# A third layer's attention: steps of two head pairs, one set of three PSUM banks for turned probabilities and projections, value products right behind the logits

## The reference, cut to what matters

```python
def _L2_attn_ref(x, qkv, out_w, rpe_bias):
    q, k, v = jnp.einsum('bsx,xMnd->Mbnsd', x, qkv)
    s = x.shape[1]
    a = jnp.einsum('bnsd,bntd->bnst', q, k) * q.shape[-1] ** (-0.5)
    cum = jnp.cumsum(rpe_bias[:, :s], axis=-1)
    rel = jnp.arange(s)[:, None] - jnp.arange(s)[None, :]
    bias = jnp.where(rel >= 0, cum[:, jnp.clip(rel, 0)], PAD)
    a = jax.nn.softmax(a + bias, axis=-1)
    mix = jnp.einsum('bnst,bntd->bnsd', a, v)
    return jnp.einsum('bnsd,ndx->bsx', mix, out_w)
```

## Time and profile before

| | us |
|---|---|
| median of 3 runs | 4019.81 (4017.57 to 4021.01) |
| the profiled execution | 4015.36 |
| its span in the trace | 4013.6 |
| the stage: first projection to last copy | 839.77 to 1426.1 |

### The profile page before, as it was taken

How to read it: one execution, slowest core, us unless ns; L and a number is a source line. 1 busy time by engine, 2 the same in 40 slices (tenths; PEclk the granted TensorE clock), 3 DMA queues, 4 the chain that set the end, 5 groups by cost and what they waited for, 6 DMA issues and landing times. The chain is left out here.

```text
span 4013.6 us, 71017 instructions
## 1 busy us (share of the span) xinstructions
PE 3466.1 (86%) x24832; PEld 2285.5 (57%) x24832; DVE 2415.3 (60%) x5406; ACT 1855.5 (46%) x5083; POOL 1704.5 (42%) x1869
## 2 busy tenths in 40 slices
PE   6888897679999989999997999979999999973681
PEld 3555554436666656666663444447777777762560
DVE  4788744346666656666653444458888888863233
ACT  4666655355666644544442000066666666630220
POOL 3555523326666643332320000036666666654106
PEclk8999998879999999999998999989999999996895
DMA  4888720120000000000006767512222222231122
GB/s 134 218 216 208 203 75 10 33 40 1 1 1 2 1 1 2 2 1 1 2 1 144 152 150 152 129 50 75 78 70 78 75 78 70 78 127 52 46 70 63
DMA packets 266185, 289.99 MB, mean 72 GB/s; under 512 B 60841, under 2 KB 177513, under 8 KB 265578
## 3 DMA queue, kind: packets, MB, share of 16 engines
q1 hardware_dynamic: 259146, 271.80, 26.8%
q0 software_dynamic: 4096, 8.40, 0.7%
q10 hardware_dynamic: 2592, 5.26, 0.3%
HBM read 233.21 MB, written 52.17 MB: 71 GB/s over the span
## 5 line engine op out<-in xcount | busy, mean ns | idle before, releaser
L2191 DVE TENSOR_TENSOR_SCAN a_h<-a_dA,a_dBu_psum 128x512 f32<-128x512 f32 x512 | 595.7, 1204 | 164.8 <-issue 106.7
L2148 POOL TENSOR_TENSOR a_h<-a_h,main_g 128x512 f32<-128x512 f32 x256 | 383.7, 1501 | 270.2 <-DVE a_h L2191 260.2
L1196 POOL TENSOR_SCALAR a_probs<-a_probs,a_row_inv 128x128 f32<-128x128 f32 (+1 forms) x512 | 381.2, 762 | 238.8 <-DVE a_row_inv L1182 238.8
L1662 DVE SCALAR_TENSOR_TENSOR m_hidden<-m_h_psum,m_gate_spread 128x512 f32<-128x512 f32 x256 | 176.7, 691 | 263.9 <-PE m_h_psum L1600 251.3
L1915 PE MATMUL a_dBu_psum<-a_B_diag,a_dt_u_turned 64*128 64x128 f32 x4096 | 316.9, 289 | 20.8 <-DVE a_h L2191 20.0
L1465 POOL TENSOR_TENSOR r_position_q<-r_turned_q 128x512 f32<-128x512 f32 x128 | 159.7, 1269 | 387.5 <-DVE r_turned_q L1510 387.5
L179 POOL TENSOR_TENSOR main_g<-main_g,main_s 128x512 f32<-128x512 f32 x28 | 41.2, 1506 | 627.4 <-ACT main_g L161 627.4
L1915 PEld LDWEIGHTS a_dBu_psum<-a_B_diag,a_dt_u_turned 64*128 64x128 f32 x4096 | 257.8, 188 | 74.8 <-issue 69.8
L1422 ACT ACTIVATE r_probs<-r_logits_psum,r_neg_max 128x256 f32<-128x256 f32 x512 | 235.0, 475 | 140.9 <-DVE r_neg_max L1516 140.9
L1936 PE MATMUL a_y_psum<-main_ident,a_h 128*128 128x128 f32 x2048 | 274.9, 276 | 7.6 <-POOL a_h L2148 6.6
L1516 DVE TENSOR_REDUCE r_neg_max<-r_logits_psum 128x2 f32<-128x512 f32 x256 | 164.8, 685 | 183.6 <-PE r_logits_psum L1332 183.6
(11 more groups left out here) (519 smaller groups left out, 7703.2 us busy)
## 6 DMA issues: line engine op xcount, KB each, us to landing
m_gate_spread<-m_gate_rows SPq DMA_DIRECT2D x64, 1024.0 KB, 8.2
main_g<-a_b_c_rows SPq DMA_DIRECT2D x256, 256.0 KB, 3.2
a_band_rows<-main_g SPq DMA_DIRECT2D x64, 512.0 KB, 3.7
a_B<-a_band_rows SPq DMA_DIRECT2D x192, 128.0 KB, 3.4
a_A<-a_band_rows SPq DMA_DIRECT2D x192, 128.0 KB, 3.2
f_x_rows<-f_zero ACTq DMA_DIRECT2D x16, 320.0 KB, 8.2
f_x_expert<-f_x_rows SPq DMA_DIRECT2D x16, 320.0 KB
f_y_rows<-f_y_expert SPq DMA_DIRECT2D x16, 320.0 KB, 2.2
```

The source lines that it names most:

```text
L1196: ins = nc.gpsimd.tensor_scalar(pr[:, h % NPR, tile[t]], pr[:, h % NPR, tile[t]], rinv[:, p % NST, q:q + 1], None, ALU.mult)
L2148: tt(h[:, r, :, :], h[:, r, :, :], Cs[:, g % NCS, :, :], ALU.mult).then_inc(hc_pool, 1)
L2191: nc.vector.tensor_tensor_scan(flat, dA[:, M % NDA, q, k, :, :].rearrange("p n t -> p (n t)"), db[:, 2 * (g % 2) + k, :], 0.0, ALU.mult, A ...
```

## The change

- The unit is two pairs of heads: 4 **double steps** for each sequence, 64 in all (`NS = NSEQ * ND`).
- The two `transposed` banks and the `project` bank become one set of three, `turned_projected`. `uses` is the list of everything that goes into it, in TensorE's order; the n-th use takes bank n % 3 and waits until use n - 3 has been copied away.
- TensorE's order in a double step `p` is: logits of both pairs of `p`; value products of both pairs of `p - 2`; then `beside(p)`, in which the transposes of the four heads of `p - 1` take turns with the projections of this step. Every double step has two q/k projections for the next sequence; the first of a sequence has two v of its own sequence (v 2 and v 3), the second the y of the last sequence, the third and the fourth one v each of the next sequence.
- `out` is filled over its 512 columns, so `keep_o` copies 512 at a time, half as often.
- ScalarE: exponentials of head 0, `keep_o`, head 1, q/k copy, head 2, q/k copy, head 3.
- VectorE: two reciprocals a double step (`invert`), for heads 0 and 1 and for heads 2 and 3. The first stands behind the copies `take(mine[1:4])` of its own step, the second behind the first `add_bias` of the next step.
- Buffers for logits, probabilities and turned probabilities: 4, 6 and 4 become 8 each. Before the first step 8 q/k and 2 v projections are made.

```diff
-        NL, NPR, NPT, NST = 4, 6, 4, 8
+        NL = NPR = NPT = 8
+        NST, NB3 = 3, 3
...
-        tb = s.banks("transposed", 2)
+        tb = s.banks("turned_projected", NB3)
         ob = s.banks("out", 1)
-        pj = s.banks("project", 1)
...
+        def projected(p):
+            b, r = p // ND, p % ND
+            todo = [("qk", b + 1, 2 * r), ("qk", b + 1, 2 * r + 1)]
+            todo += {0: [("v", b, 2), ("v", b, 3)], 1: [("y", b - 1, 0)], 2: [("v", b + 1, 0)], 3: [("v", b + 1, 1)]}[r]
+            return [job for job in todo if 0 <= job[1] < NSEQ]
+        first = [("qk", 0, n) for n in range(8)] + [("v", 0, 0), ("v", 0, 1)]
+        def beside(p):
+            heads = [("t", p - 1, i) for i in range(4)] if 1 <= p <= NS else []
+            jobs, n = projected(p), max(len(heads), len(projected(p)))
+            return [u for k in range(n) for u in heads[k:k + 1] + jobs[k:k + 1]]
+        uses = first + [u for p in range(NS + 2) for u in beside(p)]
...
+                def bank(u):
+                    n = place[u]
+                    if n >= NB3:
+                        w = uses[n - NB3]
+                        pe.wait_ge({"qk": qk_kept, "v": v_kept, "y": y_kept, "t": pt_kept}[w[0]], nth[w])
+                    return tb[:, n % NB3, :]
...
-                for p in range(NS + 4):
+                for u in first:
+                    project(u)
+                for p in range(NS + 2):
                     if p < NS:
                         logit(p)
-                    for n in at(p, 0):
-                        project(n)
-                    if 2 <= p < NS + 2:
-                        transpose(p - 2, 0)
-                        transpose(p - 2, 1)
-                    if 3 <= p < NS + 3:
-                        weigh(p - 3)
-                    for n in at(p, 1):
-                        project(n)
+                    if p >= 2:
+                        weigh(p - 2)
+                    for u in beside(p):
+                        if u[0] == "t":
+                            transpose(u)
+                        else:
+                            project(u)
...
+                    if p < NS:
+                        add_bias(p, 0)
+                    if 1 <= p <= NS:
+                        invert(p - 1, 1)
+                    if p < NS:
+                        add_bias(p, 1)
+                        add_bias(p, 2)
+                    take(mine[0:1])
+                    if p < NS:
+                        add_bias(p, 3)
+                    take(mine[1:4])
+                    if p < NS:
+                        invert(p, 0)
+                    take(mine[4:])
```

More of the change, by code:

```diff
@@ L1011, in l2_attention @@
         turned = (slice(0, T), slice(T, NK))
[L1014 to L1031, removed]
+        ND = NP2 // 2
+        NS = NSEQ * ND
+        def projected(p):
[9 more added lines that the diff above has]
+        uses = first + [u for p in range(NS + 2) for u in beside(p)]
+        place = {u: n for n, u in enumerate(uses)}
+        nth, seen = {}, {"qk": 0, "v": 0, "y": 0, "t": 0}
+        for u in uses:
+            seen[u[0]] += 1
+            nth[u] = seen[u[0]]
+        made = {u: sum(1 for w in uses[:n + 1] if w[0] != "t") for n, u in enumerate(uses)}
         def toks(b):
@@ L1037, in _, with project @@
             def _(pe):
[L1038 to L1042, removed]
+                def bank(u):
[4 more added lines that the diff above has]
+                    return tb[:, n % NB3, :]
+                def project(u):
+                    what, b, i = u
+                    pj = bank(u)
                     if what == "qk":
@@ L1062, in logit @@
[L1062 to L1070, removed]
@@ L1072, in transpose @@
-                def transpose(p, i):
-                    h = 2 * p + i
-                    pe.wait_ge(scaled, h + 1)
[L1075 to L1080, removed]
+                    b, r = p // ND, p % ND
@@ new lines, in _ @@
+                for u in first:
+                    if u[0] == "qk":
+                        keep(u)
+                for p in range(NS + 2):
+                    todo = [u for u in beside(p) if u[0] == "qk"]
+                    if p < NS:
+                        exps(p, 0)
+                    if p >= 2:
+                        keep_o(p - 2)
+                    if p < NS:
+                        exps(p, 1)
+                    for u in todo[0:1]:
+                        keep(u)
+                    if p < NS:
+                        exps(p, 2)
+                    for u in todo[1:2]:
+                        keep(u)
+                    if p < NS:
+                        exps(p, 3)
@@ L1190, in _ @@
                 for p in range(NS):
-                    pool.wait_ge(inv, p + 1)
-                    for i in range(2):
-                        h = 2 * p + i
+                    for i in range(4):
+                        h = 4 * p + i
+                        pool.wait_ge(inv, 2 * p + i // 2 + 1)
                         for t in range(2):
```

156 lines of the change are left out of this document (85 added, 71 removed).

## The result

The changed kernel takes 3959.95 us (median of 4 runs, 3958.95 to 3963.04), the kernel before 4019.93 beside it: a ratio of 0.9856 (95% interval 0.9843 to 0.9868). The medians are 60 us apart; the ratio makes it 58. The prediction said 3964, between 3951 and 3990. The profiled execution took 3963.04 us. In the rows PE is TensorE, PEld its weight loads, DVE VectorE, ACT ScalarE and POOL GpSimd.

The account below looks back on a forecast made before the run. TensorE's own order of work was taken as the bound: start -16, to first y -3, middle -38.4, fourteenth to fifteenth y -5, end +6, sum -56 off the median 4019.8, giving 3964; range 3951 to 3990.

Parts of the forecast that it names:

- Changes of group are the price, and fewer of them the gain: TensorE's steps: 0.55 us paid at changes of array split, once per double step instead of once per pair step.
- A v or y behind the value products costs 0.2 besides its streaming.: TensorE's pair steps before the change: each v or y projection behind value products costs 0.2 us beyond streaming.
- A turn between transposes and a projection costs nothing: TensorE inside a double step: switching between transposes and projections taken as 0, with 0.19 us each as the dearer end.
- rival C: Every turn between transposes and a projection costs a change, 0.19 us, 26 turns a sequence: 74 us, 4038; chance 0.05.
- GpSimd's loop at 6.99 beside 7.04: Double step with one v: GpSimd's loop from reciprocal to reciprocal takes 6.99 us, TensorE's work 7.04, so both barely fit.
- rival B: GpSimd's loop bounds the double steps: v steps 7.4 to 7.9 us, 10 to 27 us over fourteen sequences, 3974 to 3991; chance 0.28.
- The fourth head's wait: Fourth head's transposes wait for GpSimd, late by 0.2 us after a v step; 0.13 added to two of four steps.
- The start: Ten projections before the first logits: with three banks they take 11 us instead of 27.1, -16.
- The end: Last sequence, GpSimd sets the pace: fifteenth to sixteenth y 30 us instead of 23.9, +6.
- Rival D: TensorE's clock falls: a tenth of the stage at the low level costs about 50 us, 4014; chance 0.02.
- The signs: Trace checks: y period 31.9, logits at 11, last y 30, value products 1.45, turn 0.33, at most 3 us outside the stage.
- The larger buffers and the 512-column copies: Larger buffers remove waits nobody had, and ScalarE has slack for the 512-column copies of `oT`: nothing from either.

Follow-up runs that it names:

- early reciprocal: Changed kernel with VectorE's first reciprocal right behind the last head's bias, ahead of three turned copies and the projection's copy: ratio 0.9817, repeated 0.982.
- late reciprocal: Changed kernel with VectorE's first reciprocal behind all four heads' turned copies instead of ahead of the last one: ratio 0.9889 to the kernel before.
- pairs_values_later: Kernel before with three banks in turn, value products of the pair four steps back behind the logits, six turned-probability buffers: ratio 0.9964, period 35.37.
- shared scaling: Changed kernel with VectorE's first reciprocal moved early and VectorE scaling every other head of the last sequence instead of GpSimd: ratio 0.9816.

## Why the prediction was right

- *Changes of group are the price, and fewer of them the gain.* Right, shown from both sides. One-pair steps with the three banks, the value products behind the logits and v between the transposes: 33.88; doubled: 31.62, or 31.51 with the early reciprocal. (Doubling also brings larger buffers and 512-column copies of `oT`.) So doubling is worth 2.3 to 2.4, for the predicted 4 x 0.55 = 2.2, and splitting two groups costs 1.3 to 1.44 back. It is a little over 2.2 because a double step pays 0.51 and not 0.55: 4 x (1.10 - 0.51) = 2.36, for the measured 33.88 - 31.51 = 2.37. The prediction had carried over the 0.10 that a q/k projection pays behind logits; where transposes stand first it is 0.06 (0.39 for 0.33, above), and the plain double step is 7.01 and not 7.04.
- *"A v or y behind the value products costs 0.2 besides its streaming."* Right: five times 0.2 is 1.0, and moving them among the transposes brought 34.85 - 33.88 = 0.97. The value products behind the logits brought nothing by themselves in pair steps (35.37 with them, 34.85 without); in the double step the logits between are what covers the turned copies.
- *A turn between transposes and a projection costs nothing* (rival C). Right, 0.33 and 0.86.
- *GpSimd's loop at 6.99 beside 7.04* (rival B). It fits, as forecast, and how barely the late reciprocal shows: a loop of 7.4 by the prediction's own terms, and every plain v step grows to 7.32. Rival B was the right thing to fear.
- *The fourth head's wait,* "0.13 to two of the four steps": mis-sized. One step of four has it, 0.11 (7.12 for 7.01). Early, both are 7.01. So the period was 31.62 and not 31.9, 3.6 us over thirteen sequences. The end and its last y gave 2.5 of that back, and the prediction's parts add up to -56.4 where the stage gave -58.6. That the whole came so near owes something to luck: these two errors offset each other.
- *The start:* 10.3 instead of 11. The clock rose as it had behind the v projection; the eight q/k projections took 8.5 us.
- *The end:* +6.7 for +6, by the mechanism given: the reciprocal moved early takes 5.5 of it back. But the clock at the end was left out, and it cost 1.8. Rival D looked for it between 875 and 1350, where it stayed at 1.00. The Trainium skill, in "TensorE: Matmul & The Clock Gate" ("A second HAM failure mode: psum-queue depth-cycling"), reports a kernel whose clock swung between its two levels as it cycled through PSUM banks. This trace shows no such swing, at 1.00 over 455 us with three banks in turn.
- *The signs.* Steps, start, end and the turn came within 0.7 us of what was named; only "value products 1.45 behind the logits" was a slip, it is 1.51, the figure that the prediction's own sum for the fourth head uses. The last sign, anything outside the stage moving by more than 3 us, was met by the letter, with 5.0 behind the stage. It was drawn too narrow: one execution differs from another by that much in code that nobody touched.
- *The larger buffers and the 512-column copies:* nothing, as said, as far as the steps add up without them; they weren't tried alone.

## What to carry over

When an engine is busy without a gap and its groups take longer than their streaming, list the starts and count the changes of group. Larger groups then pay in proportion, if other work covers what the group in front needs and if banks are cycled in the order of use. When a group is moved, follow its hand-over on the other engine too: what stands ahead of the copy that frees its bank may stand behind the moved group itself. A loop of durations that sums to the step is strong evidence, and opening the loop, as here, is the proof.

## What the runs showed of the hardware

- The price of a change depends on which groups meet (from one group's start to the next's, over bare streaming): transposes to logits 0.09, q/k to transposes 0, value products to transposes 0.15, logits to value products 0.21. The 0.20 of a v has two halves. In the kernel before, where v stands behind value products, from v to the logits is 1.06; in the changed kernel the second v of a sequence stands behind transposes, with no change of split ahead of it, and it is 0.96 (1075.42 to 1076.38), the same at all fourteen such places between 880 and 1330 us. So 0.10 is paid on leaving for the logits, as behind transposes, and 0.10 by a v that is itself the first behind a change, as by a q/k behind logits (0.96) against one behind transposes (0.86). A v that had just waited for its bank paid it too (1.06 in `pairs_values_later`). The Trainium skill, in "TensorEngine Tiling (Array Packing)" (Key Properties), says that changing the tiling mode drains TensorE. The trace agrees in that each change has its price, 0.09 to 0.21, and q/k to transposes, where the mode stays, has none; the draining itself no row shows.
- The clock fell in the last steps of the changed kernel, where TensorE waits for GpSimd head by head. Windows of 9 us, the changed kernel, then the early reciprocal, then one window of the shared scaling:

```profile
1343.00:1352.00 9.00, 5.63 (x47) 3.68 (x47) 5.36 (x25) 4.56 (x19) 6.43 (x9) 1.00 0.02 4
1352.00:1361.00 9.00, 6.59 (x39) 4.41 (x41) 2.38 (x7) 0.60 (x1) 5.94 (x8) 0.74 0.00 0
1361.00:1370.00 9.00, 6.97 (x26) 5.20 (x23) 0.43 (x1) 0.60 (x1) 0.00 (x0) 0.70 0.00 0
```

```profile
1343.00:1352.00 9.00, 6.68 (x45) 4.60 (x42) 4.13 (x15) 3.82 (x14) 8.76 (x12) 0.81 0.01 3
1352.00:1361.00 9.00, 6.27 (x38) 4.89 (x38) 1.21 (x3) 0.60 (x1) 0.00 (x0) 1.00 0.00 0
```

```profile
1343.00:1352.00 9.00, 5.38 (x49) 3.85 (x47) 5.49 (x18) 3.08 (x12) 3.30 (x4) 1.00 0.01 3
```

  And the late reciprocal, windows and then its last y:

```profile
1361.00:1370.00 9.00, 5.78 (x33) 3.90 (x31) 3.54 (x12) 3.57 (x14) 7.63 (x11) 0.81 0.01 3
1370.00:1379.00 9.00, 6.25 (x33) 4.55 (x34) 1.44 (x3) 0.60 (x1) 1.77 (x3) 0.81 0.00 0
1376.68 3.69 PE L1065 MATMUL 22_turned_projected_psum<-a_oT,a_wo 128*128 128x256 f32 x16 [0.78 <-ACT a_oT L1132]
```

  After nine microseconds in which TensorE had only 5.6 us of matmuls, its clock went from 1.00 to 0.74 and 0.70, a mean of the two levels, and the last y ran mostly at 1.2 GHz. With the early reciprocal it dipped once (0.81) and was back for the last y. That this is due to its shorter waits isn't shown. The late reciprocal has the same waits of 0.93 for GpSimd as the changed kernel, and its clock dips twice, yet its last y takes 3.69, at full clock. The shared scaling has 5.38 us of matmuls in nine and stays at 1.00. Among the kernels with double steps the last y ran slow in three (5.48 in the changed kernel, 5.96 with two banks, 5.46 with the value products first) and took 3.69 in the others. So waits at the end of a stage can cost twice, their own length and slower work behind them; whether the dip meets the last y is a matter of a few microseconds, and the 1.8 us may be luck of that kind.
